# Eight single stores in place of two pairs and four singles, in a gathered 64 x 64 matmul with residual

## What is computed

```python
w = weights[conditions]                       # (64, 64, 64) from (200, 64, 64)
x = x + jnp.einsum('bct,bcd->bdt', x, w)      # (64, 64, 512)
```

## Time and profile before

| what | value |
|---|---|
| median of 3 runs | 46.11 us (46.01 to 48.03) |
| the profiled execution, its time | 46.19 us |
| span of the profiled execution | 44.9 us |
| PE busy | 31.0 us (69%) |
| VectorE busy | 15.1 us (34%) |
| ScalarE busy | 13.4 us (30%) |
| bytes moved by DMA | 17.83 MB, mean 397 GB/s |
| granted TensorE clock | 1.0 of full speed |

### The profile page before, as it was taken

One profiled execution on the slowest core, in us unless ns is written; L12 is line 12 of the kernel. 1 busy time (PEld: TensorE's weight loads), 2 busy tenths in 40 slices (PEclk: granted clock), 3 DMA queues, 4 the chain that ended last, 5 costly groups with the idle time before them and its releaser, 6 DMA issues.

```text
span 44.9 us, 331 instructions
## 1 busy us (share of the span) xinstructions
PE 31.0 (69%) x100; PEld 13.4 (30%) x100; DVE 15.1 (34%) x24; ACT 13.4 (30%) x16; POOL 1.6 (4%) x9
## 2 busy tenths in 40 slices
PE   0040000499999979999999699999999999920000
PEld 0040000433534144543453235344354453300000
DVE  1220000000009990758730490085086073063000
ACT  0894000000000064736710480085085071062000
POOL 4008100000000000000000000000000000000000
PEclk9999999999999999999999999999999999999999
DMA  0389999999999899999995989999998999999993
GB/s 0 81 314 431 424 431 431 424 431 431 416 438 519 372 467 467 467 467 467 438 467 248 438 380 424 409 453 438 424 424 372 409 424 424 431 424 394 402 438 153
DMA packets 1730, 17.83 MB, mean 397 GB/s; under 512 B 194, under 2 KB 194, under 8 KB 194
## 3 DMA queue, kind: packets, MB, share of 16 engines
q1 hardware_dynamic: 1584, 16.78, 89.2%
q0 software_dynamic: 144, 1.05, 5.5%
q10 hardware_dynamic: 2, 0.00, 0.0%
HBM read 9.44 MB, written 8.39 MB: 397 GB/s over the span
## 4 chain that ended last, share of the span: by engine, by line
DMA 50%; PE 31%; SPq 4%; DVE 3%; issue 1%; POOLq 0%
DMA x_sb<-x 50%; PE product L166 31%; SPq L94 4%; DVE y_sb L216 3%; POOLq L134 0%
## 5 line engine op out<-in xcount | busy, mean ns | idle before, releaser
L166 PE MATMUL product<-x_sb,w_diag 128*128 (+1 forms) x40 | 17.7, 597 | 0.4 <-POOLq L134 0.4
L216 DVE COPY y_sb<-product 128x1024 f32<-128x1024 f32 x8 | 9.8, 1224 | 12.9 <-PE product L166 10.5
L117 ACT COPY y_sb<-product 128x1024 f32<-128x1024 f32 x8 | 8.1, 1012 | 13.6 <-PE product L166 11.3
L146 PE MATMUL product<-x_sb 128*128 128x512 f32 x10 | 7.3, 907 | 5.4 <-DMA x_sb<-x 5.4
L166 PEld LDWEIGHTS product<-x_sb,w_diag 128*128 128x128 f32 x40 | 7.4, 190 | 10.5 <-issue 10.5
L158 PE MATMUL product<-x_sb,w_all 64*64 64x512 f32 x48 | 5.5, 601 | 0.3 <-DVE w_all L205 0.3
L146 PEld LDWEIGHTS product<-x_sb 128*128 128x128 f32 x10 | 2.9, 302 | 9.1 <-issue 9.1
L111 ACT COPY w_diag<-w_all 64x256 f32<-64x256 f32 x1 | 0.6, 642 | 12.3 <-DVE w_all L205 12.3
L202 DVE TENSOR_TENSOR gathered<-gathered,piece 128x64 f32<-128x64 f32 x1 | 0.3, 267 | 10.2 <-DMA gathered<-weights,table_row 10.2
L158 PEld LDWEIGHTS product<-x_sb,w_all 64*64 64x64 f32 x48 | 2.5, 200 | 3.3 <-issue 2.1
L205 DVE STREAM_TRANSPOSE w_all<-gathered 128x2048 f32<-128x2048 f32 x1 | 2.3, 2311 | 0.0
(11 more groups left out here) (9 smaller groups left out, 1.6 us busy)
## 6 DMA issues: line engine op xcount, KB each, us to landing
x_sb<-x SPq DMA_DIRECT2D x4, 1024.0 KB, 9.3
x_sb<-x SPq DMA_DIRECT2D x1, 4096.0 KB, 22.7
out<-y_sb SPq DMA_DIRECT2D x2, 2048.0 KB, 8.0
out<-y_sb SPq DMA_DIRECT2D x4, 1024.0 KB, 5.4
condition<-conditions ACTq DMA_DIRECT2D x1, 0.2 KB
gathered<-weights,table_row POOLq DMA_INDIRECT x1, 9.8
```

Source lines behind the costliest of these rows:

```text
L117: nc.scalar.copy(y_sb[:, 4 * turn:4 * turn + 2, :], product[turn % SETS][0][:, :, :]).then_inc(moved_by_act, 1)
L146: nc.tensor.matmul(product[1][0][:, 0, :], x_sb[:, 0, 0:P], x_sb[:, 0, :], start=True, stop=True)
L166: product_of = nc.tensor.matmul(product[s][j][:, g, :], w_diag[:, s, 2 * j + g, :], x_pair(2 * j + g), start=True, stop=True)
L216: nc.vector.tensor_copy(y_sb[:, 4 * turn + 2:4 * turn + 4, :], product[turn % SETS][1][:, :, :]).then_inc(moved_by_dve, 1)
```

## The change

The list of stores becomes one entry for each turn. It was turns 0 and 1 together, turns 2 and 3 together, and turns 4, 5, 6 and 7 singly.

```diff
     LOADS = [(0, 0), (1, 1), (2, 2), (3, 3), (4, 7)]
-    STORES = [(0, 1), (2, 3), (4, 4), (5, 5), (6, 6), (7, 7)]
+    STORES = [(turn, turn) for turn in range(TURNS)]
```

## The result

The changed kernel takes 46.27 us in the median (22 runs, 45.92 to 48.1), the kernel before 46.03 us beside it (22 runs). The ratio is 1.0039, with a 95% interval of 1.0022 to 1.0056: 0.18 us slower, between 0.10 and 0.26. The ratio leaves out one run of each kernel (48.03 and 48.1 us), in a slower state of the chip that comes with any kernel. The forecast was 0.1 us slower, 46.2 us; the sign agrees, and the forecast size is at the low end of the interval.

A forecast was written before the change was run, and what follows sets the result against it. Two chains were taken to end together: load, PE, move, last store; and the store stream. Terms +0.1 + 0 + 0 + 0 = +0.1 us on a 46.11 us median gave 46.2 us, range 45.9 to 46.8.

The forecast's parts named there:

- What bounds the kernel: At the end two limits meet: load, PE, move and last store; and the store stream. Gaining in one is almost worthless.
- Packets: Stores of turns 0 to 3: 512 packets of 8 KB for 256 of 16 KB, between 0 and +0.21 us, taken as +0.1.
- Issues: On SyncE, four store issues of 0.33 to 0.35 us in place of two, hidden under PE's turns 3 and 4: 0.
- Turn 2 leaves earlier: Turn 2's store is issued at about 23.7, not 26.56, but joins a backlog with no idle time to fill: 0.
- The load: At the load's end, the earlier store should not delay the landing that releases PE: 0.
- No price at all: Rival: the store stream's added packets cost nothing and the time stays at 46.1 us; chance 0.27.
- The fixed cost for every transfer: Rival: each of the two added store transfers shows 1.5 us on the path, 49.1 us; chance 0.05.
- The third store in the load's tail: Rival: turn 2's store delays the load's landing, 46.9 us if shared half and half, 48.5 at worst; chance 0.07.
- Earlier work for the engines: Rival: new issues fill idle parts of 0.18 us behind the load and 0.04 before turn 7, 45.9 us; chance 0.06.
- What would show it: Signs in the trace: issue times, load landing at 25.4, PE's 14.0 us, about 420 GB/s, landings 2.4 us apart, last at 44.9.
- clearly over 4 us: Sign against the forecast: turn 7's store taking this long from issue to landing, where it took 3.9 us before.

The follow-up runs named there:

- the doses: Ten timings of kernels with -8 to 80 data packets more an engine than the kernel before; a fitted line gives 7 ns a packet, 0.11 us for the change.
- the eight transfers of 4 KB: Kernel before, with turns 0 to 3 stored in eight transfers of 0.5 MB with 4 KB runs: 46.45 us, ratio 1.0074 (with four transfers 46.56 us, 1.0095).
- the late third store: Changed kernel, with turn 2's store waiting for turn 3's moves: 46.09 us, ratio 1.0009; timed again 46.23 us, ratio 1.0028, both ratios against the kernel before.
- the kernel with 4 KB everywhere: Changed kernel, with every turn's store as two transfers of 4 KB runs, 16 transfers in all: 46.72 us, ratio 1.0113 against the kernel before.
- the kernel with the second pair split: Kernel before, with turns 0 and 1 still one store and turns 2 and 3 stored singly: 46.21 us, ratio 1.0012.

## Why the prediction was right

- **What bounds the kernel.** Shown: with one store gone the end stands 0.2 us ahead of the kernel before and 0.4 ahead of the changed one, not 2.45; with the issue of turn 7's first half 0.3 us sooner it moves by nothing measurable; with 80 packets more an engine it moves back by 0.5. The prediction's sentence that a delay of the stream reaches the end and a gain in one limit is worth almost nothing held in all three.
- **Packets, +0.1 us.** The term was chosen halfway between 0 (landings) and 0.21 (rates), and the doses give 0.11. The change itself measured 0.18 and 0.08. The mechanism was right; that the size came out so close was luck. The upper bound had no firm base: 429 against 420 is within the spread of such rows, since the changed kernel reads 420 in one execution and 427 in another. The average of the two bounds was a choice, not a measurement, and it was the runs of 4 KB and the lengths of the packets that gave the size.
- **Issues, 0.** The cost was right, a part of the reason was not. The third issue lasts 0.87 us and not 0.35. It ends at 24.59 and nothing waits for it: turn 3's move ends at 26.4. The cover that was named is what hides it.
- **Turn 2 leaves earlier, 0.** Nothing else was measured, to within 0.1 us, by the pair timed side by side: 46.17 with it early, 46.23 with it late.
- **The load, 0.** It landed at 25.30, not later than before.
- **No price at all** stays possible for a single run of this size (the second measurement's interval begins at 0.9999), but not for the mechanism, which grows with the dose.
- **The fixed cost for every transfer** fell with the eight transfers of 4 KB, which cost no more than the four. The Trainium skill's fit of 2.0 us plus bytes ("DMA: Bandwidth & Descriptors", section "Anatomy of one DMA — SWDGE (gpsimd) path") was measured on GpSimd's path. Here something of its shape shows only at the last store, with nothing queued behind it (1.5 us beyond the movement, not 2.0); in a queue, transfers of 1 MB landed 2.4 to 2.5 us apart.
- **The third store in the load's tail** fell with the load's landing and with the late third store. **Earlier work for the engines** brought no gain, as its rows said.
- **What would show it.** Named ahead: landings 2.4 us apart and unchanged PE (seen), 420 GB/s up to 33.9 (seen in one trace, 427 in the other), turn 7's landing at 44.9 (45.0), and "clearly over 4 us" from issue to landing as a sign against. It took 4.2. That sign was badly chosen: with the issue fixed by PE, any delay of the stream must show in exactly this number.

## What to carry to other kernels

Where a queue of stores is never empty, the number of transfers was free here and the number of packets was not: count the contiguous runs an engine has to move, here at about 7 ns each, and lengthen the runs where turns are ready together anyway. Where two chains end together, price a change on each of them, and expect losses to show and gains on one side almost not at all. A cost near what can be measured is sized by experiments that multiply it (here by three and by five), not by repeating it.

## What the runs showed of the hardware that was not expected

Stores over half of the partitions: the same bytes and the same runs of 8 KB as the changed kernel, but 64 partitions at a time, made the kernel 11.4% slower than the kernel before, at 324 GB/s with the engines 0.98 busy, then at 353 with 1.00. The Trainium skill ("DMA: Bandwidth & Descriptors", section "Rules for kernel authors") advises one transfer over 128 partitions in place of two over disjoint halves, because both halves use the same sixteen engines and serialize. The trace agrees on the sixteen engines and adds the price: they were all busy and yet moved a sixth to a quarter less than the 420 to 430 of the full transfers. Why a packet takes longer there was not tried.

Issues of stores on SyncE mostly lasted 0.33 to 0.38 us when few came close together, and much longer when several small ones followed one another: 0.87 for turn 2 in the changed kernel, 1.19 for turn 3 when turn 2's came right ahead of it, mostly 1.2 to 1.3 in the kernel with 4 KB everywhere, and up to 2.40 in the kernel with halves of the partitions. Two rows, of these last two kernels in turn:

```profile
27.04 1.26 SPq L103 DMA_DIRECT2D out<-y_sb  x1
...
24.72 2.40 SPq L102 DMA_DIRECT2D out<-y_sb  x1
```

1.26 us is what the stream needs for 0.5 MB at that kernel's 415 GB/s, so an issue seems to wait for room behind the stores ahead of it. How the room is counted stays open. It is not the queued bytes (0.38 us with 3 MB queued in the kernel with the second pair split), nor simply the number of unfinished transfers: turn 3's issue at 26.47 in the changed kernel lasted 0.33 us, when turns 0 to 2 had not landed yet. In the changed kernel it cost nothing, since SyncE had nothing else to do. With halves of the partitions it held turn 7's last store back to 44.70, 4 us behind the last move, and only the full stream hid that.
